# Attention with an interleaved scan: the running sum of 16 states on GpSimd in SBUF in place of GpSimd pairs and TensorE accumulation in PSUM

## What is computed

```python
# layer 2 attention: B=4, 512 queries, 512 keys, 16 heads of 128, rms-normed q and k
scores = jnp.einsum('bqhd,bkhd->bhqk', q, k) * scale
attn = jax.nn.softmax(scores, axis=-1)
out = jnp.einsum('bhqk,bkhd->bqhd', attn, v)
return out.reshape(B, Sq, H * D) @ Wo

# layer 3 recurrence: 512 channels, 16 states each, 512 steps
def step(state, inp):
    d, b, c, u = inp
    dA = jnp.exp(d[..., None] * A)
    state = state * dA + (d * u)[..., None] * b[:, None, :]
    y = jnp.einsum('bdn,bn->bd', state, c)
    return (state, y)
y = y + D[None, :, None] * x
```

## Time and profile before

| what | value |
|---|---|
| three runs | 3847.47, 3850.71, 3865.67 us; median 3850.71 |
| the profiled execution | 3872.61 us, of which the profile's span is 3870.9 us |
| the stage of the change | 1578 to 3028 us of the span: 1450 us |
| busy in the whole span | PE 88%, PEld 51%, DVE 68%, ACT 45%, POOL 29% |
| mean granted clock of PE | 0.923 of 2.4 GHz |
| `collect` on PE | 128 products, recorded as 256 instructions, 139.0 us busy |
| `add_pair` on POOL | 128 additions, 192.2 us busy, 1501 ns in the mean |
| `inflows` on POOL | 256, 409.5 us busy, 1600 ns in the mean |
| scan and gather on DVE | 256 each, 399.5 us and 201.8 us busy, 1561 and 788 ns in the mean |

### The profile page before, as it was taken

The page is one execution under the profiler, slowest core; times in us unless marked ns, Lnnn a source line. Parts: engine busy times, 40 slices in busy tenths (PEclk is TensorE's granted clock), DMA queues, the critical chain, the costliest instruction groups (busy, mean ns, idle before and its releaser), DMA issues. The chain is left out here.

```text
span 3870.9 us, 42977 instructions
## 1 busy us (share of the span) xinstructions
PE 3388.3 (88%) x14533; PEld 1966.7 (51%) x14564; DVE 2614.0 (68%) x3658; ACT 1758.4 (45%) x3362; POOL 1110.6 (29%) x814
## 2 busy tenths in 40 slices
PE   5858888999987877999999999999998799999526
PEld 2337644333335554555555555555554588877423
DVE  5844688777748886567767777777777432256578
ACT  4643243656644444655555555555554112155310
POOL 0120177000000000445444545545544224312100
PEclk9978899799999999999999999999998789999758
DMA  3023544222228001444444444444433513367511
GB/s 98 34 109 131 195 113 117 60 57 55 61 82 120 1 1 42 139 133 130 142 132 126 151 136 133 135 138 153 135 128 106 139 30 101 101 214 247 181 54 44
DMA packets 237232, 426.23 MB, mean 110 GB/s; under 512 B 40015, under 2 KB 73423, under 8 KB 229600
## 3 DMA queue, kind: packets, MB, share of 16 engines
q1 hardware_dynamic: 230784, 406.79, 35.0%
q0 software_dynamic: 6240, 16.81, 1.1%
HBM read 345.58 MB, written 81.59 MB: 110 GB/s over the span
## 5 line engine op out<-in xcount | busy, mean ns | idle before, releaser
L2263 POOL TENSOR_TENSOR l2x_inflow<-l2x_dtu,l2x_rows_b 128x512 f32<-128x512 f32 x256 | 409.5, 1600 | 591.8 <-DVE l2x_state L2156 555.9
L179 POOL TENSOR_TENSOR ln_work<-ln_work,minus_half 128x4 f32<-128x4 f32 x33 | 33.4, 1012 | 1353.9 <-DVE ln_work L167 1353.8
L2156 DVE TENSOR_TENSOR_SCAN l2x_state<-l2x_decay,l2x_inflow 128x512 f32<-128x512 f32 x256 | 399.5, 1561 | 18.2 <-ACT l2x_decay L2033 18.2
L1222 DVE TENSOR_REDUCE l1x_mx<-psum 128x2 f32<-128x1024 f32 x256 | 308.3, 1219 | 112.9 <-PE psum L1064 111.3
L1976 ACT ACTIVATE l2x_probs<-psum,l2x_soft,l2x_norms 128x512 f32<-128x512 f32 x256 | 195.8, 774 | 335.1 <-DVE l2x_soft L2097 335.1
L1179 ACT ACTIVATE l1x_split<-psum 128x1024 f32<-128x1024 f32 x256 | 262.1, 1025 | 171.2 <-PE psum L1064 171.1
L126 PE MATMUL psum<-l2x_probs_t,l2x_v_tok 128*128 128x512 f32 x512 | 235.2, 602 | 12.0 <-ACT l2x_probs_t L212 11.0
L126 PE MATMUL psum<-l2x_xt,l2x_wq 128*128 128x512 f32 x512 | 230.1, 593 | 0.6 <-issue 0.2
L126 PE MATMUL psum<-l2x_kt,l2x_qt 128*128 128x512 f32 x512 | 230.2, 592 | 0.0
L126 PE MATMUL psum<-l2x_wo,l2x_ot 128*128 128x512 f32 x512 | 225.1, 592 | 0.8 <-ACT l2x_ot L212 0.8
L2033 ACT ACTIVATE l2x_decay<-l2x_dt,a_neg 128x512 f32<-128x512 f32 x256 | 180.3, 717 | 76.7 <-DVE l2x_state L2156 76.7
(11 more groups left out here) (392 smaller groups left out, 7440.1 us busy)
## 6 DMA issues: line engine op xcount, KB each, us to landing
l2x_rows_b<-l3x_xd_dram SPq DMA_DIRECT2D x256, 256.0 KB, 3.8
l2x_rows_c<-l3x_xd_dram SPq DMA_DIRECT2D x256, 256.0 KB, 3.3
l1x_heads_dram<-l1x_stage SPq DMA_DIRECT2D x32, 512.0 KB, 3.3
l2x_wq<-l_wq SPq DMA_DIRECT2D x16, 1024.0 KB, 8.2
l2x_wo<-l_wo SPq DMA_DIRECT2D x16, 1024.0 KB, 5.3
l2f_xs_dram<-l1f_empty SPq DMA_DIRECT2D x1, 11799.0 KB, 88.6
l2r_xs<-l2f_xs_dram SPq DMA_DIRECT2D x23, 513.0 KB, 3.8
l2r_raw<-l_w SPq DMA_DIRECT2D x11, 1024.0 KB, 7.0
```

The source lines that it names most:

```text
L1222: main.drain(dve.tensor_reduce(mx[:, gg % 2, :, j, t], g["psum"][:, b:b + 2, :], AX.X, ALU.max), f"m{n}_0", banks=2)
L2156: dve.tensor_tensor_scan(state[:, s % KEPT, :], decay[:, s % 3, :], inflow[:, s % 3, :], 0.0, ALU.mult, ALU.add).then_inc(scan_done, 1)
L2263: pool.tensor_tensor(inflow[:, s % 3, :], dtu[:], rows_b[:, s % 3, :], ALU.mult).then_inc(inflow_ready, 1)
```

## The change

`collect` and `y_bank` go. POOL adds each gathered state to a running sum `y_sum` in SBUF (one buffer per unit, two in turn): the first addition of a unit adds states 0 and 1, and each of the 14 others adds one state, so it makes 15 additions in a unit where it made 8. Each addition waits for the one before it. The skip term reads `y_sum` in place of the PSUM bank. The ring of the attention has all eight banks. To make room, `k_sq`, a scratch output of ACT, has one buffer in place of two. A scan may reuse a state's buffer once POOL has added it.

```diff
-        k_sq, q_sq = sb("k_sq", [P, 2, S]), sb("q_sq", [P, 4, S])
+        k_sq, q_sq = sb("k_sq", [P, S]), sb("q_sq", [P, 4, S])
...
+        y_sum = sb("y_sum", [P, 2, S])
...
-        jobs += [(f"spare{k}", None) for k in range(-len(jobs) % 7)]
-        ring = Ring(sem, "l2x", range(7), jobs)
-        y_bank = g["psum"][:, 7, :]
+        jobs += [(f"spare{k}", None) for k in range(-len(jobs) % 8)]
+        ring = Ring(sem, "l2x", range(8), jobs)
...
-            def collect(u, m):
-                if u >= 0:
-                    k = u * NS // 2 + m
-                    pe.wait_ge(paired, k + 1)
-                    if m == 0:
-                        since(pe, y_read, u)
-                    pe.matmul(y_bank, g["ident"][:], state[:, 2 * k % KEPT, :], start=(m == 0),
-                              stop=(m == NS // 2 - 1)).then_inc(y_filled, 1)
-
             for u in range(-1, NU):
                 score(u, 0)
-                collect(u - 1, 6)
                 x_turned(u + 1)
                 context(u + 1, "k", wk, wk_in, (0, 1))
-                collect(u - 1, 7)
...
-                    since(dve, y_filled, (s - KEPT) // 2 + 1)
+                    since(dve, added, s - KEPT + (2 if n == 0 else 1))
...
-                    dve.wait_ge(y_filled, (u + 1) * NS // 2)
+                    dve.wait_ge(added, (u + 1) * NS)
                     tile = u_in[:, u % 2, :]
-                    dve.scalar_tensor_tensor(tile, tile, g["skip"][:, u % G2:u % G2 + 1], y_bank, ALU.mult,
+                    dve.scalar_tensor_tensor(tile, tile, g["skip"][:, u % G2:u % G2 + 1], y_sum[:, u % 2, :], ALU.mult,
                                              ALU.add).then_inc(y_read, 1)
...
-            def add_pair(u, n):
+            def add_state(u, n):
                 if n < 0:
                     u, n = u - 1, n + NS
-                if u >= 0 and n % 2:
-                    s = u * NS + n
-                    pool.wait_ge(gathered, s + 1)
-                    even = state[:, (s - 1) % KEPT, :]
-                    pool.tensor_tensor(even, even, state[:, s % KEPT, :], ALU.add).then_inc(paired, 1)
+                if u < 0 or n == 0:
+                    return
+                s = u * NS + n
+                total = y_sum[:, u % 2, :]
+                pool.wait_ge(gathered, s + 1)
+                if n == 1:
+                    since(pool, y_read, u - 1)
+                    pool.tensor_tensor(total, state[:, (s - 1) % KEPT, :], state[:, s % KEPT, :], ALU.add
+                                       ).then_inc(added, 2)
+                else:
+                    pool.wait_ge(added, s)
+                    pool.tensor_tensor(total, total, state[:, s % KEPT, :], ALU.add).then_inc(added, 1)
```

More of the change, by code:

```diff
@@ L1754, in l2_xattn @@
              "k_scaled", "q_ms", "q_norm", "pool_steps", "max_ready", "bias_ready", "inv_ready", "probs_ready")]
-        (dtu_ready, decay_ready, inflow_ready, scan_done, gathered, y_filled, y_read) = [sem(n) for n in (
-            "dtu_ready", "decay_ready", "inflow_ready", "scan_done", "gathered", "y_filled", "y_read")]
-        paired = sem("paired")
+        (dtu_ready, decay_ready, inflow_ready, scan_done, gathered, added, y_read) = [sem(n) for n in (
+            "dtu_ready", "decay_ready", "inflow_ready", "scan_done", "gathered", "added", "y_read")]
         dt_in, u_loaded, y_out = [[sem(f"{n}{k}") for k in range(2)] for n in ("dt_in", "u_loaded", "y_out")]
@@ L1940, in _ @@
                 query(u + 1, 0)
-                collect(u, 0)
                 turn(u, 0)
@@ L1945, in _ @@
                 turn(u, 1)
-                collect(u, 1)
                 score(u, 2)
@@ L1949, in _ @@
                 query(u + 1, 2)
-                collect(u, 2)
                 turn(u, 2)
@@ L1953, in _ @@
                 query(u + 1, 3)
-                collect(u, 3)
                 value(u, 2)
@@ L1957, in _ @@
                 turn(u, 3)
-                collect(u, 4)
                 value(u, 3)
@@ L1962, in _ @@
                 output(u, (0, 1))
-                collect(u, 5)
                 output(u, (2, 3))
-            collect(NU - 1, 6)
-            collect(NU - 1, 7)
         @blk.scalar
@@ L2001, in context @@
                                 cols = slice(h * P, (h + 1) * P)
-                                act.activation(k_sq[:, t % 2, cols], bank(f"k{u}_{t}")[:, cols], ACT.Square,
+                                act.activation(k_sq[:, cols], bank(f"k{u}_{t}")[:, cols], ACT.Square,
                                                accum_out=norms[:, u % 2, 2, h, t:t + 1]).then_inc(k_squared, 1)
@@ L2276, in _ @@
                     inflows(u, n)
-                    add_pair(u, n - 1)
+                    add_state(u, n - 1)
                     if n == 3:
@@ L2283, in _ @@
                         query_norms(u + 1)
-            add_pair(NU - 1, NS - 1)
+            add_state(NU - 1, NS - 1)
 E2, I2 = 8, 256
```

## The result

After the change the kernel takes **3896.72 us** in the median of 4 runs (3891.03 to 3916.73), before 3852.09 (4 runs). The ratio is 1.0119, with the interval 1.0074 to 1.0165: slower by 44.6 us, where 42 were predicted.

What follows compares the result with a forecast made beforehand. DVE was taken to bound each unit up to head 2's transposes, PE the rest. 15 units x (2.4 - 1.7 + 2.1) = +42, less 3, plus 3: 3850.7 + 42 = 3893 us, range 3842 to 3925.

Steps and rivals of the forecast that it cites:

- DVE sets stretch A: From a unit's first scores to head 2's transposes (42.2 us in unit 8), DVE's list sets the time, not PE.
- Additions in A, +2.4 a unit: Before head 2's transposes, new POOL additions cost DVE 2.7 us a unit, less 0.3 of slack: +2.4 us.
- Collects 3 and 5 paid for, 4 not, -1.7: Between head 2's transposes and the next scores, two of three removed collects save 0.86 us each: -1.7 us a unit.
- The slow restart, +2.1 a unit: PE, idle 7 us before head 2's transposes, restarts at half clock for 4.2 us: +2.1 us a unit.
- Stretch B 48 us: From head 2's transposes to the next unit's scores, set by PE: 47.5 - 1.7 + 2.1 = 48 us.
- The last unit +3: Last unit, nearly all set by DVE: 2.7 and some 2 us for additions, less 1.7 for two collects: +3 us.
- A wait at turn 2 in every unit: PE waits at the transposes of head 2 in every unit, 6 to 8 us each.
- PE busy less by 110: PE's busy time in the stage falls by about 110 us, without shortening the stage.
- Scans and gathers longer by 0.1 to 0.15 each: DVE's scans and gathers, 1561 and 788 ns before, grow in the mean by 0.1 to 0.15 us each.
- PE as the bound: Rival: PE bounds the whole stage, all 128 collects count, 110 us, giving 3741; chance 0.12 together with a milder form.
- The idle PE that costs nothing: Rival: PE's clock doesn't fall, or is back at its restart; +10 us, 3861, no measurable change; chance 0.19.
- POOL more often in the way: Rival: all four additions before head 2's transposes cost DVE in full, 5.0 us a unit; +80 us, 3930; chance 0.12.

Runs made afterwards that it cites:

- Experiment 1: Changed kernel with the additions of the even states from 2 on left out, so 8 additions a unit and no collects: 3823.02 us, ratio 0.9912.
- Experiment 4: Changed kernel with a seven-bank ring, plus ten unread PE products in its wait before the transposes of head 2: 3853.59 us, ratio 1.0007.
- experiment 5: Changed kernel with the same 15 additions a unit, moved to places where DVE is expected to read PSUM or wait: 3809.08 us, ratio 0.9908.
- experiment 9: Changed kernel with 14 of the 15 additions a unit doing only 256 of 512 columns: 3818.39 us, ratio 0.9909.
- experiment 2: Changed kernel with a seven-bank ring and two unread 256-column PE products at each of the eight old collect places: 3892.01 us, ratio 1.0095.
- experiment 7: Changed kernel with the additions of states 4 and 6, and 7 with them, moved behind the inflow of step 10: 3894.8 us, ratio 1.0115.
- experiment 8: Kernel before the change with only the addition of the pair of states 4 and 5 moved behind the inflow of step 10: 3851.56 us, ratio 0.9997.
- experiment 3: Changed kernel with a ring of seven banks, the eighth left empty: 3889.22 us, ratio 1.0085.

## Why the prediction was right

It gave 3893, +42 us, and the way there was mostly the one named; that the number came within 3 us is in part luck, as the terms show. Means are over units 0 to 14.

**DVE sets stretch A: right in twelve units of fifteen.** There 4.3 us less of PE's work in A didn't shorten it. Experiment 1 shows the same without the additions: A goes from 43.45 only to 43.01 in the mean. That fall is all of units 3, 7 and 11 (44.44 to 42.16), and the other twelve stay in the mean (43.21 and 43.22). In those three PE came last before: turn 2 followed the normalisation by 0.57 to 0.98 us, and PE didn't wait for it. The prediction had seen the 0.98, and averaged it to 0.3.

**Additions in A, +2.4 a unit: right in sum and in unit 8, wrong in how it is spread.** The terms were 1.9 in the run and 0.8 on the normalisation, less 0.3. In unit 8 the run grew by 1.78 and the normalisation by 0.60, of which 0.25 was caught by a start that came as much sooner: 2.13, and A grew by 2.1. The mean over all units is +2.03. But the units are of three kinds. The eight ordinary ones grew by 1.90 in the mean, 0.5 less than given. Units 3, 7 and 11, with PE's transposes of x, grew by 0.05 in place of 1.4: DVE's wait at maxima 1 went, and PE's late arrival at turn 2 with it, more than the 1 us given, so that their A is now 44.5, near the 44.2 of the ordinary ones. And units 2, 6, 10 and 14 grew by **3.76**, from 45.0 to 48.7, for which the sum had 2.4. There DVE's adding of the output to the residual (line 218) stands among the scans at the start of the unit. Unit 6 before and after, scan 0, scan 1 and the maxima of head 0:

```profile
2127.03 1.22 DVE L2156 TENSOR_TENSOR_SCAN l2x_state<-l2x_decay,l2x_inflow 128x512 f32<-128x512 f32 x1
...
2130.22 2.19 DVE L2156 TENSOR_TENSOR_SCAN l2x_state<-l2x_decay,l2x_inflow 128x512 f32<-128x512 f32 x1
2132.34 1.85 DVE L2090 TENSOR_REDUCE l2x_soft<-psum 128x1 f32<-128x512 f32 x3
```

```profile
2118.71 2.19 DVE L2136 TENSOR_TENSOR_SCAN l2x_state<-l2x_decay,l2x_inflow 128x512 f32<-128x512 f32 x1
...
2122.86 2.20 DVE L2136 TENSOR_TENSOR_SCAN l2x_state<-l2x_decay,l2x_inflow 128x512 f32<-128x512 f32 x1
2124.99 1.26 DVE L2070 TENSOR_REDUCE l2x_soft<-psum 128x1 f32<-128x512 f32 x2
```

The unit's scores start at 2127.65 before and at 2118.45 after. So the maxima of head 0 start 4.69 us behind them before and 6.54 after: the whole 1.9 us by which this unit grew more than the ordinary ones stands there already. 0.97 of it is scan 0, now held beside an addition on POOL (at 2118.56). The other 0.88 lies ahead of scan 0, which started 0.62 us before the scores and now starts 0.26 behind them; that PE's scores come earlier against DVE's list is my reading, without a run for it. I had worked the sum out for unit 8 alone and multiplied by 15; the misses nearly cancel (8 x 0.5 and 3 x 1.35 us too much, 4 x 1.36 too little: 2.6 in all). That is luck.

**Collects 3 and 5 paid for, 4 not, -1.7: right** (44.2 against 45.93 in experiment 1).

**The slow restart, +2.1 a unit: right, by a wrong idle time.** What the lower clock costs in B, taken against the B that has none, went from 2.07 to 3.9 us a unit, so +1.8. Experiment 4 takes away the part at turn 2. The rows behind turn 2 (0.58 against 1.00) show it directly. 1.3 of the 1.8 us lie between turn 2 and the scores of head 3 (3.06 against 1.77), the rest later in B. But I had PE idle for 7 us at turn 2, and the mean is 3.5. Part of the 4.3 us of PE's early arrival is spent sooner; in unit 8 it waits 2.08 us ahead of value 1:

```profile
2331.65 3.70 PE L126 MATMUL psum<-l2x_probs_t,l2x_v_tok 128*128 128x512 f32 x8 [2.08 <-ACT l2x_probs_t L212]
```

The shortest stop that I had priced was of 5.5 us; this one of 3.7 was followed by the lower clock as well. There the clock was 1.00 for the first 0.5 us of turn 2 and then 0.50 for 3.4. In 11 of the 15 units PE fell to the lower level behind its restart, by up to 1.3 us, and didn't restart at it, as the prediction had it.

The Trainium skill, TensorE: Matmul & The Clock Gate, Part 1, says that the throttled clock is the default and activity releases it. After the stop of 3.7 us the trace agrees with it; after those of 0.65 to 1.3 us in the mean in experiments 1, 5 and 9 no slow restart is seen.

**Stretch B 48 us: right** (48.10; before 48.00). **The last unit +3: measured +4.7** (83.6 against 78.9). So the stage's 36.5 us are 30.5 (A), 1.5 (B) and 4.7.

**The signs given.** Stage +40: 36.5. Scan 5 to maxima 2 10.5 us: 10.40. A wait at turn 2 in every unit: yes, but of 2.1 to 3.9 us in place of 6 to 8. A fall of the clock at every turn 2: in all 15. PE busy less by 110: only 63, because more of it runs at half speed and is longer (174 us at the lower clock, before 82). Scans and gathers longer by 0.1 to 0.15 each: half wrong. The scans are not longer (1514 ns, before 1561), the gathers are (972, before 788), and so is the normalisation (735 a tile over all heads, before 660). In the rows of unit 8 the addition is released by a gather or by the inflow ahead of it, when the next scan has begun, and it meets the gather after that.

**The rivals.** PE as the bound falls by experiments 1 and 2. The idle PE that costs nothing falls by experiment 4. POOL more often in the way was said of stretch A at 5.0 us a unit; the growth was 2.03 in the mean, and only units 2, 6, 10 and 14, with 3.76, show something of it.

The time of the profiled execution before lay 22 us above the median. I took the difference over to the median; the two profiled executions differ by 18.4 us only (3891.03 - 3872.6), since the surplus of that of before lies ahead of the stage: its first scores came at 1578 us, here at 1562. The median of before leaves 3852.1 - 1450.7 = 2401.4 us outside the stage, the profiled execution after 3891.0 - 1487.2 = 2403.8. So the stage's 36.5 us are the change, and the 5.7 us by which after's median lies above its profiled execution make most of the rest of the 44.6. For the stage alone the forecast was 5.5 us too high, and the executions' scatter brings the medians near to it.

The Trainium skill, SBUF — State Buffer, section Who interferes with whom, calls the port pair that DVE and GpSimd share an exclusive lock. By that an addition would have cost DVE its whole 1.26 us. The gathers show 0.88 to 0.90: most of it, with 0.4 us overlapped.

## What to carry to other kernels

A step that is taken from a full engine gives only what lies on the stretches that this engine ends: here two collects of eight, and some more in three units. A GpSimd addition of two SBUF tiles must be charged to VectorE where it meets a gather (0.88 of its 1.26 us here), so place it beside reads of PSUM, whose 2.48 us didn't grow, or in VectorE's waits; look at where it lands, since a late DMA can push it off that place (experiments 5, 7 and 8). And before an engine is relieved, ask what it does with the time: the longer stop of TensorE cost 1.8 us a unit in clock here, and the two collects that paid saved 1.7.

## What the runs showed that I had not expected

- Unread products in TensorE's longest wait gave 36 us (3889.22 to 3853.59), 21 of them at turn 2. The other part is that a fall around turn 3, behind the sixteen one-column products of `query_norms`, stayed away in 8 of 15 units. Before has it in 14 units, experiment 3 in all 15, experiment 5 in 9. Why is open.
- Stops of 3.5 us in the mean ahead of turn 2 (after) were followed by the lower clock, and from turn 2 to the scores of head 3 it took 3.06 us; behind stops of 0.65 to 1.3 us in the mean at the same place (experiments 1, 5 and 9) it took 1.80. Between them the length of the stop alone didn't decide: of twelve stops of 2.05 to 2.13 us in experiment 2 five were followed by a slow turn 2 (2.58 to 3.19 us), and the one of 2.5 us in experiment 1 (unit 9) wasn't.
- Two kernels with the same instructions on every engine, after and experiment 5, differ by 88 us by the places of fifteen additions alone.
